# A decoder layer on one core: row sums with the residual, squares on ScalarE, normalization factors on GpSimd, and a reordered feed-forward

## The reference

```
x = layernorm(x + hyena(x))                  # long convolution, untouched here
x = layernorm(x + cross_attention(x, ctx))   # 16 heads of 16, 64 context rows a batch
x = layernorm(x + ffn(x))
layernorm(x) = (x - mean(x)) / sqrt(var(x) + 1e-5)          # over 256 columns
bitlinear(x, w) = act_quant(x) @ weight_quant(w).T          # 8-bit rows, ternary weights
act_quant(x): scale = 127 / clip(max|x| over the row, 1e-5); round(x * scale) / scale
ffn(x) = bitlinear(silu(bitlinear(x, w_gate)) * bitlinear(x, w_up), w_down)   # inner 1024
```

## Time and profile before

| | us |
|---|---|
| median of three runs | 913.16 |
| profiled execution, its own time | 915.69 |
| its span, first to last instruction | 913.7 |
| TensorE busy | 722.2 (79%) |
| VectorE busy | 682.6 (75%) |
| ScalarE busy | 361.2 (40%) |
| GpSimd busy | 339.2 (37%) |

### The profile page before, as it was taken

The page is one execution under the profiler, slowest core; times in us unless marked ns, Lnnn a source line. Parts: engine busy times, 40 slices in busy tenths (PEclk is TensorE's granted clock), DMA queues, the critical chain, the costliest instruction groups (busy, mean ns, idle before and its releaser), DMA issues. The chain is left out here.

```text
span 913.7 us, 12328 instructions
## 1 busy us (share of the span) xinstructions
PE 722.2 (79%) x4407; PEld 517.4 (57%) x4422; DVE 682.6 (75%) x1299; ACT 361.2 (40%) x600; POOL 339.2 (37%) x439
## 2 busy tenths in 40 slices
PE   2699899977989779879759439898899846877783
PEld 0285674766658665667547325476777633444452
DVE  3853888899878996989887410178888847998895
ACT  2224427021374016440133135645665634545452
POOL 0220443545148431675126204503310013556475
PEclk9999999989999899999979759979999998999998
DMA  8100424423043813343000866000000000000102
GB/s 303 35 1 0 93 47 93 92 22 25 1 92 70 154 8 58 58 116 46 1 1 27 172 182 230 1 1 2 1 2 2 2 0 1 1 25 24 46 25 70
DMA packets 33465, 48.59 MB, mean 53 GB/s; under 512 B 4506, under 2 KB 28059, under 8 KB 33149
## 3 DMA queue, kind: packets, MB, share of 16 engines
q0 software_dynamic: 7392, 15.72, 11.5%
q1 hardware_dynamic: 26012, 32.09, 10.6%
HBM read 27.89 MB, written 8.39 MB: 40 GB/s over the span
## 5 line engine op out<-in xcount | busy, mean ns | idle before, releaser
L536 ACT ACTIVATE yb<-banks 128x256 f32<-128x256 f32 x64 | 24.3, 386 | 233.5 <-PE banks L361 176.4
L352 PE MATMUL banks<-inv_m,spec_y 128*128 128x256 f32 x384 | 87.6, 381 | 8.0 <-POOL spec_y L618 8.0
L388 PE MATMUL banks<-xt_in,w_in 128*128 128x512 f32 x192 | 84.1, 593 | 2.1 <-ACT spec_h L500 1.3
L352 PEld LDWEIGHTS banks<-inv_m,spec_y 128*128 128x128 f32 x384 | 72.3, 190 | 20.8 <-POOL spec_y L618 11.3
L316 PE MATMUL banks<-z_cplx,fwd_m 128*128 128x256 f32 x240 | 73.8, 390 | 8.0 <-DVE prod L818 8.0
L325 PE MATMUL banks<-z,fwd_m 128*128 128x256 f32 x176 | 52.5, 465 | 32.0 <-POOL z L636 16.2
L617 POOL TENSOR_TENSOR spec_y<-prod 128x256 f32<-128x256 f32 x64 | 49.8, 777 | 68.5 <-DVE prod L818 67.3
L317 PE MATMUL banks<-z_cplx,fwd_m 128*128 128x256 f32 x240 | 73.2, 387 | 0.0
L325 PEld LDWEIGHTS banks<-z,fwd_m 128*128 128x128 f32 x176 | 41.3, 240 | 45.8 <-issue 26.9
L1534 ACT ACTIVATE silu<-ps_gate,gate_back 128x1024 f32<-128x1024 f32 x32 | 35.7, 1114 | 66.1 <-issue 39.3
L388 PEld LDWEIGHTS banks<-xt_in,w_in 128*128 128x128 f32 x192 | 36.0, 190 | 45.1 <-issue 43.3
(11 more groups left out here) (218 smaller groups left out, 1763.0 us busy)
## 6 DMA issues: line engine op xcount, KB each, us to landing
x_t<-left POOLq DMA_DIRECT2D x16, 511.5 KB, 5.2
xt_in<-in_x_t SPq DMA_DIRECT2D x4, 1024.0 KB, 6.7
x_tok<-in_x SPq DMA_DIRECT2D x8, 512.0 KB, 4.4
x_tok<-in_b_out POOLq DMA_DIRECT2D x8, 512.0 KB, 12.6
x_scratch<-x_tok SPq DMA_DIRECT2D x8, 512.0 KB, 3.8
x<-x_scratch SPq DMA_DIRECT2D x8, 512.0 KB, 7.6
out<-x SPq DMA_DIRECT2D x8, 512.0 KB, 2.9
v_t<-left POOLq DMA_DIRECT2D x6, 511.5 KB, 5.4
```

The costliest lines, as they stand in the source:

```text
L352: last = mm(bank[:, odd * 2 * P:(odd + 1) * 2 * P], spec_y[:, j + odd, part * D + h * P:part * D + (h + 1) * P], inv_m[:, o:o + 2 * P], st ...
L388: last = mm(proj_pair(t)[:, c * 512:(c + 1) * 512], w_in[:, k, TILES[t] * P:(TILES[t] + 1) * P], xt_in[:, k, c * 512:(c + 1) * 512], start ...
```

## The change

In attention and feed-forward alike:

- `row_stats` and `aggregate` are gone from VectorE. The residual is added by an instruction that also gives the row's sum. In attention that is one instruction for each tile where there was one for a pair.
- ScalarE squares (row sum - 256 x) and sums over the row. In attention two squares stand in every even j from 6 on (pair j/2-3), in feed-forward `square(s-4)` is at the end of slot s.
- GpSimd makes the factors from both sums with four small instructions. Factors and sums have two buffers.
- In attention GpSimd also normalizes, in chunks 0 to 6; ScalarE does the last one only.
- In feed-forward TensorE runs `down(s-3)` behind the gate product, where `down(s-2)` stood at the slot's end. `x_scales` moves from s % 4 == 0 to s % 4 == 1. GpSimd normalizes tile s-8 instead of s-7. The last chunk gets its factors, its normalization and its store tile by tile.

```diff
 # attention
+            def squares(i):                                             # ScalarE
+                act.wait_ge(added, i + 1)
+                for j in (2 * i, 2 * i + 1):
+                    c, k = j // CH, j % CH
+                    if j:
+                        act.wait_ge(squared, j)
+                    if c >= 2:
+                        act.wait_ge(floored, c - 1)
+                    fn(spread_sq[:], x2[:, j, :], ACT.Square, scale=-float(D), bias=row_sum[:, c % 2, k:k + 1],
+                       accum_out=row_var[:, c % 2, k:k + 1]).then_inc(squared, 1)
...
-                if j % CH == 2 and j >= 10:
-                    norm_chunk(j // CH - 2)
-            norm_chunk(CHUNKS - 2)
+                if j % 2 == 0 and j >= 6:
+                    squares(j // 2 - 3)
+            squares(HALVES - 3)
             evac_inverses(HALVES - 1)
-            norm_chunk(CHUNKS - 1)
+            squares(HALVES - 2)
+            squares(HALVES - 1)
+            norm_last(CHUNKS - 1)
...
             def norm_factors(c):                                        # GpSimd
+                h = c % 2
+                pool.wait_ge(squared, CH * (c + 1))
+                if c >= 2:
+                    pool.wait_ge(x2_ready, c - 1)
+                nc.gpsimd.tensor_scalar(rstd[:, h], row_var[:, h], 1.0 / D ** 3, LN_EPS, ALU.mult, ALU.add)\
+                    .then_inc(floored, 1)
+                nc.gpsimd.tensor_scalar(mean_neg[:, h], row_sum[:, h], -1.0 / D, 1.0, ALU.mult, ALU.mult)\
+                    .then_inc(centred, 1)
+                pool.wait_ge(floored, c + 1)
+                nc.gpsimd.tensor_tensor(rstd[:, h], rstd[:, h], half_neg[:], ALU.pow).then_inc(raised, 1)
...
+            def norm_chunk(c):
+                norm_factors(c)
+                pool.wait_ge(shift_ready, c + 1)
+                for k in range(CH):
+                    x = x2[:, c * CH + k, :]
+                    last = nc.gpsimd.tensor_scalar(x, x, rstd[:, c % 2, k:k + 1], shift_by[:, c % 2, k:k + 1],
+                                                   ALU.mult, ALU.add)
...
             def add_residual(i):                                        # VectorE
-                tt(rows, ps_ctx[:].rearrange("p (k n) -> p k n", k=2), rows, ALU.add).then_inc(added, 1)
+                    if c >= 2 and k == 0:
+                        dve.wait_ge(squared, CH * (c - 2) + m + 2)
+                        dve.wait_ge(centred, c - 1)
+                    last = stt(x2[:, j, :], ps_ctx[:, k * D:(k + 1) * D], 1.0, x2[:, j, :], ALU.mult, ALU.add,
+                               accum_out=row_sum[:, c % 2, m:m + 1])
...
 # feed-forward, TensorE
-            for s in range(-1, TILES_ALL + 2):
+            for s in range(-1, TILES_ALL + 3):
                 if s + 1 in tiles:
                     inner(s + 1, ps_gate, w_gate, silu_done, gate_mm)
+                if s - 3 in tiles:
+                    down(s - 3)
...
                     inner(s + 1, ps_up, w_up, h_ready, up_mm)
-                if s - 2 in tiles:
-                    down(s - 2)
...
 # ScalarE
                     evac_x(s + 2)
+                if s - 4 in tiles:
+                    square(s - 4)
...
 # GpSimd (norm_factors as above, over columns k0 to k1)
-                done = s - CH - 3
+                done = s - CH - 4
...
+            for k in range(CH):
+                norm_factors(CHUNKS - 1 + k, CHUNKS - 1, k, k + 1)
+                norm(CHUNKS - 1 + k, TILES_ALL - CH + k)
...
 # VectorE
-                if s - 3 in tiles:
-                    row_stats(s - 3)
-                if s in tiles:
                     hidden_scale(s)
-                if s % CH == 2 and s >= CH + 2:
-                    aggregate(s // CH - 1)
-                if s % CH == 0 and s // CH + 2 < CHUNKS:
+                if s % CH == 1 and s // CH + 2 < CHUNKS:
                     x_scales(s // CH + 2)
...
 # SyncE
+            for c in range(CHUNKS - 1):
+                store(c * CH, (c + 1) * CH)
+            for i in range(TILES_ALL - CH, TILES_ALL):
+                store(i, i + 1)
```

More of the change, by code:

```diff
@@ L1293, in _ @@
                 add_bias(c)
+            def norm_chunk(c):
[5 more added lines that the diff above has]
+                                                   ALU.mult, ALU.add)
+                last.then_inc(x2_ready, 1)
             def quantize(i, dst):
@@ L1307, in _ @@
                 if i < 2:
-                    norm_factors(i)
-            for c in range(2, CHUNKS):
-                norm_factors(c)
+                    norm_chunk(i)
+            for c in range(2, CHUNKS - 1):
+                norm_chunk(c)
+            norm_factors(CHUNKS - 1)
         @block.vector
@@ L1354, in add_residual @@
                 dve.wait_ge(biased, 2 * i // CH + 1)
-                rows = x2[:, 2 * i:2 * i + 2, :]
-                tt(rows, ps_ctx[:].rearrange("p (k n) -> p k n", k=2), rows, ALU.add).then_inc(added, 1)
-            def row_stats(i):
-                dve.wait_ge(added, i + 1)
                 for k in range(2):
[L1361 to L1377, removed]
+                    j = 2 * i + k
+                    c, m = j // CH, j % CH
+                    if c >= 2 and k == 0:
[3 more added lines that the diff above has]
+                               accum_out=row_sum[:, c % 2, m:m + 1])
+                last.then_inc(added, 1)
             for j in range(TILES_ALL):
@@ L1386, in _ @@
                         invert(i)
[L1387 to L1394, removed]
+                elif i >= 1:
+                    normalize(i - 1)
             normalize(HALVES - 2)
@@ L1456, in _, with store @@
         def _(sp):
[L1457 to L1461, removed]
+            def store(i0, i1):
+                sp.wait_ge(out_ready, i1)
+                sp.dma_start(out[i0 * P:i1 * P, :].rearrange("(t p) n -> p t n", p=P), x2[:, i0:i1, :])\
+                    .then_inc(st_out, 16)
+            for c in range(CHUNKS - 1):
+                store(c * CH, (c + 1) * CH)
+            for i in range(TILES_ALL - CH, TILES_ALL):
+                store(i, i + 1)
+            sp.wait_ge(st_out, 16 * (CHUNKS - 1 + CH))
         @block.tensor
@@ L1541, in evac_hidden, with square @@
                 fn(hq_t[:, i % 2].rearrange("p t n -> p (t n)"), ps_ht[:].bitcast(I16), ACT.Copy).then_inc(ht_evac, 1)
+            def square(i):
+                act.wait_ge(added, i + 1)
+                c, k = i // CH, i % CH
+                if i:
+                    act.wait_ge(squared, i)
+                if c >= 2:
+                    act.wait_ge(floored, c - 1)
+                fn(spread_sq[:], x2[:, i, :], ACT.Square, scale=-float(D), bias=row_sum[:, c % 2, k:k + 1],
+                   accum_out=row_var[:, c % 2, k:k + 1]).then_inc(squared, 1)
             evac_x(0)
-            for s in range(-1, TILES_ALL + 2):
+            for s in range(-1, TILES_ALL + 4):
                 if s + 1 in tiles:
@@ L1610, in _ @@
                     round_x(s + 3)
-                done = s - CH - 3
+                done = s - CH - 4
                 if done >= 0:
+                    c = done // CH
                     if done % CH == 0:
-                        norm_factors(done // CH)
-                    norm(done)
-            for i in range(TILES_ALL - CH - 3, TILES_ALL):
+                        norm_factors(c, c, 0, CH)
+                    norm(c, done)
+            for i in range(TILES_ALL - CH - 4, TILES_ALL - CH):
+                c = i // CH
                 if i % CH == 0:
-                    norm_factors(i // CH)
-                norm(i)
+                    norm_factors(c, c, 0, CH)
+                norm(c, i)
+            for k in range(CH):
+                norm_factors(CHUNKS - 1 + k, CHUNKS - 1, k, k + 1)
+                norm(CHUNKS - 1 + k, TILES_ALL - CH + k)
         @block.vector
@@ L1666, in add_residual @@
                 dve.wait_ge(back_down, i + 1)
[L1667 to L1688, removed]
+                c, k = i // CH, i % CH
+                if c >= 2:
+                    dve.wait_ge(squared, CH * (c - 2) + k + 1)
+                    dve.wait_ge(centred, c - 1)
+                stt(x2[:, i, :], ps_down[i % 2][:, 0:D], down_back[:, k:k + 1], x2[:, i, :],
+                    ALU.mult, ALU.add, accum_out=row_sum[:, c % 2, k:k + 1]).then_inc(added, 1)
             nc.vector.tensor_copy(ident[:], ident_f[:]).then_inc(ident_ready, 1)
```

64 lines of the change are left out of this document (32 added, 32 removed).

## The result

| us | before | after |
|---|---|---|
| median of the runs | 913.16 | 886.11 |
| profiled execution / its span | 915.69 / 913.7 | 885.35 / 883.4 |
| VectorE, TensorE busy | 682.6, 722.2 | 649.8, 714.2 |
| ScalarE, GpSimd busy | 361.2, 339.2 | 383.0, 362.5 |

Ratio 0.9708, 95% interval 0.968 to 0.9736: 3% faster; 889 was forecast. The ratios here compare undisturbed executions with those of the kernel before on the same chip; the profiled executions of `e1_attention_only` and `e3_row_stats_even` were disturbed, so no stage is read from those two.

A forecast was written before the change was run, and what follows sets the result against it. Bounds taken: attention's pair loop containing `row_stats`; in feed-forward VectorE in at least the long slots, afterwards the ring. Attention -7.7, feed-forward -22.0, tail +5.3 sum to -24.4 from 913.16: 889 us, own range 884 to 894.

The forecast's parts named there:

- Attention, -7.9: Attention: `row_stats` leaves the loop of the tile pairs, -0.61 us in each of 13 pairs.
- Squares, residual at 0: Attention: two squares on ScalarE and two residual instructions on VectorE fit into existing waits, cost 0.
- VectorE's slots: Feed-forward: plain slot 3.1 us on VectorE, `x_scales` adds 1.86; four tiles need 14.3, 3.57 each.
- rival B: Feed-forward slots of about 4.07 us from VectorE's waits or GpSimd's late `round_x`: +8.6, 898; chance 0.23.
- the ring: Feed-forward: a loop through TensorE and ScalarE, gate product to next gate product, sets 3.75 us a slot.
- the one slot in four with `x_scales` is absorbed: Feed-forward: VectorE averages 3.57 us and `hidden` may come some 1.3 late, so the long slot costs nothing.
- Moving `down`, 0.33 a slot: Feed-forward: `down` behind the gate product shortens the slot that waits for the evacuation, 4.08 us, by 0.33.
- rival E: Feed-forward: the moved `down` does nothing and the tail grows, +8.9 us; chance counted within rival B.
- Moving `x_scales`: Feed-forward: a slot later `x_scales` no longer waits 0.93 us for `round_x`, so it costs 1.86, not 2.79.
- Tail, +5.3: Last `hidden` to the end: GpSimd's queue of factors and normalizations makes 16.8 us into 22.1; lower end +2.
- C: Attention pairs stay at 8.99 us because squares delay the odd tile's exponential: +7.9, 897; chance 0.11.
- D, the other side: Feed-forward: ScalarE's table loads alternate between `Silu` and `Square`, 5.6 us a slot: +50, 939; chance 0.06.

The follow-up runs named there:

- e1_attention_only: Attention of the changed kernel with the feed-forward of the kernel before: 905.07 us, ratio 0.9889.
- e3_row_stats_even: The kernel before with `row_stats` moved to the other half of the attention pair, nothing removed: 912.02 us, ratio 0.9964.
- e12: The kernel before with `row_stats` in the even half, run once more to see its stages: 909.07 us in one execution.
- e11: The changed kernel with a second, unused square ahead of each of attention's squares: 892.04 us, ratio 0.9769.
- e6: The changed kernel with the four-column floor of `x_scales` split into four one-column instructions: 885.96 us, ratio 0.9709.
- e4: The changed kernel with `down(s-2)` back at the end of the slot: 895.43 us, ratio 0.978.
- e5: The changed kernel with `x_scales` back at s % 4 == 0: 886.9 us, ratio 0.9725.

## Why the prediction was right

- **Attention, -7.9:** right in mechanism; -10.1 in the traces. 13 pairs gave 0.65 each: 0.61 of `row_stats` and about 0.04 by shorter peaks (1.16, 1.21 before). The term left out is the last interval, -0.84: `norm_chunk` on ScalarE had delayed an exponential there, and I had written 0. The turn waited 1.28 for it in the kernel before (rows below) and 0.44 in the kernel after. The remaining 0.78, the first pair, is the clock's. I had priced `aggregate` at 0 from pairs where the statistics stood in the other half; e12 shows that beside them it costs 9.48 - 8.34 = 1.14 a pair.

```profile
730.20 2.06 ACT L1257 ACTIVATE x<-x,a_shift,a_rstd 128x256 f32<-128x256 f32 x4
...
732.17 1.04 ACT L1239 ACTIVATE prob<-prob 128x1024 f32<-128x1024 f32 x1
...
733.27 1.09 PE L1137 MATMUL ps_pt<-ident,prob 128*128 128x128 f32 x8 [1.28 <-ACT prob L1239]
```

- **Squares, residual at 0:** right. e11 measured the cover of the squares, 0.4 us.
- **VectorE's slots:** a plain one is 3.21, forecast 3.1; `x_scales` adds 2.49 (5.70 - 3.21), forecast 1.86. The hold is 0.86 of it (1.03 - 0.17), which I had seen as "small VectorE operations sometimes stretch" and priced only in rival B. So VectorE needs 15.34 for four slots and not 14.3, more than the ring's 15.0, and the pattern of four that I had said would be absent is there. The step "the one slot in four with `x_scales` is absorbed" held up to s = 9 and failed for 13, 17 and 21, which cost 0.10, 0.35 and 0.35.
- **The ring, 3.75:** right in mechanism and size. It set 24 of the 27 intervals of `down` in the kernel after and all 27 in e6; the mean slot behind the start-up is 3.763. That the loop is only 32 tiles long is luck: from s = 17 on VectorE sets the chunk, and a longer loop would go on at 3.83 a slot (an estimate from 15.34 / 4). The start-up took 13.46, forecast 13.2.
- **Moving `down`, 0.33 a slot:** shown by e4, 8.25 where rival E had 8.9. **Moving `x_scales`:** I had credited 0.93 a chunk; e5 shows no gain behind the start-up, and there 1.1 at most once the clock is set aside.
- **Tail, +5.3:** +2.6. Direction and queue were right; the terms mis-sized are the power on one column (0.55 and not 1.01, by which a set of factors with its normalization takes 2.04 and not 2.44: 4 x 0.4 = -1.6), and the store of a quarter of the bytes, -1.2. The lower bound given, +2, covered it.
- **Rivals:** B's stretched VectorE operation showed once a chunk from s = 9 on and cost 0.8 in all, where B had 0.32 in each slot; TensorE waited for GpSimd's `xq_f` only 0.9 us in 780:850. C did not happen. D, the other side, is out: no load beyond 1. The rule cited there from the Trainium skill ("ScalarE: Activation LUTs", Table sets) does not list square among the fillers; the trace has one load over 32 SiLUs and 32 squares in turn, so it cost nothing here.

Without the clock's 1.6 and 0.8 the errors are -1.4 in attention, +0.5 in feed-forward and -2.7 in the tail: -3.6. The time came out 2.9 below the forecast.

## What to carry to other kernels

Price a removed instruction by where it stands in the loop, and ask of each neighbour whether its own cover is then gone too: moving `row_stats` beside `aggregate` brought 3.3 us, removing both 10 with the rest of attention's change. Work out every bound of a stage, not the lowest alone: here the ring (15.0) and VectorE (15.34) were 2% apart, and removing VectorE's excess brought 0.4 us. Count how often each bound sets an interval on the engine that all tiles pass: the period of an engine that has a lead is not the stage's. And look at the clock of a stretch before its time is put down to an edit. Splitting the last chunk for an early store pays only if the engine that makes the factors isn't the one that is late.

## What the runs showed of the hardware

- A 128x4 `tensor_scalar` on VectorE was held until GpSimd's instruction ended. Four of the eight L1669 began beside `round_hidden`: they took 521, 867, 1023 and 1029 ns, the others 169 or 170. One on 128x1 was not: in e6 all 16 that ran beside `round_hidden` took 143 to 156 ns. The Trainium skill ("Advanced Engine Details and Errata", VectorE Performance Modes) notes that VectorE's second SBUF port is shared with GpSimd and that two-port instructions and GpSimd's block each other; the trace agrees for the 128x4, and why the 128x1 is spared was not tried.
- GpSimd's power takes 0.55 us on one column, 0.86 on three, 1.02 on four.
- A store of 128 KB lands in 1.7 us, one of 512 KB in 2.9.
- With the granted clock at 0.51 (1.2 GHz) the four matmuls of a gate product took 1.91 us (e5), at 1.00 they take 1.04.
